# Output copies a unit later, key rounded first in the step, output and value projections between late scores and early transposes

## The reference, cut to what matters

```python
x = x + 0.5 * ffn(layernorm(x))    # router, top 2 of 8 experts, silu, projection, rms norm
x = x + attn(layernorm(x))
x = x + 0.5 * ffn(layernorm(x))
# attn: 16 query heads, 4 key and value heads of 128
q, k = apply_rope(x @ wq.T), apply_rope(x @ wk.T) * key_weights;  v = x @ wv.T
scores = where(causal, -inf, q @ k.T * 128 ** -0.5)
out = (softmax(scores) @ v) @ wo.T
```

## Time and profile before

| what | us |
| --- | --- |
| median of 3 runs | 860.69 |
| lowest, highest | 859.84, 865.01 |
| the profiled execution | 858.07 |
| its span | 856.3 |
| TensorE busy | 787.0 (92%) |
| VectorE busy | 630.1 (74%) |
| ScalarE busy | 531.2 (62%) |
| GpSimd busy | 512.6 (60%) |

### The profile page before, as it was taken

How to read it: one execution, slowest core, us unless ns; L and a number is a source line. 1 busy time by engine, 2 the same in 40 slices (tenths; PEclk the granted TensorE clock), 3 DMA queues, 4 the chain that set the end, 5 groups by cost and what they waited for, 6 DMA issues and landing times.

```text
span 856.3 us, 15659 instructions
## 1 busy us (share of the span) xinstructions
PE 787.0 (92%) x4520; PEld 671.5 (78%) x4520; DVE 630.1 (74%) x1888; ACT 531.2 (62%) x1314; POOL 512.6 (60%) x408
## 2 busy tenths in 40 slices
PE   7899999778999999999999999999999988899996
PEld 4688878657888888878888788887888867788885
DVE  6889895786666766667666676666766677989876
ACT  3565556667667676676766767667676664544543
POOL 4645569764867768677686776867767651103212
PEclk9999999789999999999999999999999999999999
DMA  8235502111123112122211312122121110000001
GB/s 299 94 105 184 198 13 63 26 25 38 26 74 90 32 37 73 37 52 71 73 25 37 105 29 74 37 61 58 41 73 25 38 25 1 1 1 26 1 26 49
DMA packets 30629, 50.11 MB, mean 59 GB/s; under 512 B 3970, under 2 KB 12802, under 8 KB 30594
## 3 DMA queue, kind: packets, MB, share of 16 engines
q1 hardware_dynamic: 30596, 49.71, 20.6%
HBM read 18.76 MB, written 9.96 MB: 34 GB/s over the span
## 4 chain that ended last, share of the span: by engine, by line
POOL 27%; PE 25%; DVE 18%; issue 15%; ACT 12%; DMA 1%; DVEq 1%; POOLq 0%; ACTq 0%; SPq 0%
POOL at_rot L1307 7%; POOL gc L1305 7%; POOL at_rot L1303 6%; POOL at_ql L1295 4%; DVE at_pth L1430 4%; ACT at_pr L1607 3%; ACT at_pr L1598 3%; PE sc L985 3%; PE sc L987 3%; PE sc L986 3%; DVE at_pr L1417 3%; POOL at_keys L1295 2%; DVE at_ptl L1436 2%; DVE f_acc L500 2%; PE pt L1785 1%
## 5 line engine op out<-in xcount | busy, mean ns | idle before, releaser
L1598 ACT ACTIVATE at_pr<-at_pr,at_low 128x512 f32<-128x512 f32 (+7 forms) x256 | 134.5, 526 | 126.5 <-DVE at_low L1417 126.5
L1430 DVE CAST at_pth<-pt 128x512 fp32r<-128x512 f32 x192 | 106.1, 594 | 34.9 <-PE pt L1785 34.8
L1607 ACT ACTIVATE at_pr<-at_pr,at_inv 128x512 f32<-128x512 f32 (+7 forms) x256 | 119.1, 525 | 13.6 <-DVE at_inv L1424 12.1
L1295 POOL TENSOR_TENSOR at_ql<-at_rot,at_qh 128x512 fp32r<-128x512 f32 x64 | 82.6, 1290 | 73.3 <-ACT at_qh L1557 73.3
L1442 DVE TENSOR_TENSOR at_ol<-o,at_oh 128x512 fp32r<-128x512 f32 x64 | 44.1, 689 | 109.3 <-ACT at_oh L1611 109.2
L1305 POOL TENSOR_TENSOR gc<-gc,sin 128x512 f32<-128x512 f32 x80 | 103.7, 1297 | 19.8 <-DMA gc<-ga 19.8
L1307 POOL TENSOR_TENSOR at_rot<-at_rot,gc 128x512 f32<-128x512 f32 x80 | 103.3, 1291 | 6.3
L1417 DVE CUSTOM_DVE_ANT_0 at_pr<-sc,at_mask 128x512 f32<-128x512 f32 (+2 forms) x192 | 91.7, 519 | 19.1 <-PE sc L1772 19.1
L1303 POOL TENSOR_TENSOR at_rot<-ga,cos 128x512 f32<-128x512 f32 x80 | 103.6, 1295 | 2.3 <-POOL at_ql L1295 2.3
L1436 DVE TENSOR_TENSOR at_ptl<-pt,at_pth 128x512 fp32r<-128x512 f32 x192 | 104.9, 587 | 0.0
L1785 PE MATMUL pt<-ident,at_pr 128*128 128x128 f32 x640 | 88.5, 277 | 16.5 <-DVE at_ptl L1436 13.6
(11 more groups left out here) (279 smaller groups left out, 2204.3 us busy)
## 6 DMA issues: line engine op xcount, KB each, us to landing
gc<-ga SPq DMA_DIRECT2D x160, 128.0 KB, 2.3
ga<-in_attn_w SPq DMA_DIRECT2D x8, 384.0 KB, 5.0
at_wo<-attn_split SPq DMA_DIRECT2D x6, 512.0 KB, 4.2
attn_split<-gb SPq DMA_DIRECT2D x6, 384.0 KB, 2.4
attn_split<-gc SPq DMA_DIRECT2D x6, 384.0 KB, 3.3
gb<-attn_split SPq DMA_DIRECT2D x6, 384.0 KB, 3.5
x<-in_x SPq DMA_DIRECT2D x4, 512.0 KB, 8.9
e_raw<-in_expert_w SPq DMA_DIRECT2D x8, 256.0 KB, 5.8
```

The lines of the kernel that those rows point to most:

```text
L1295: pool.tensor_tensor(to, rotated(r), lead.bitcast(F32), ALU.subtract).then_inc(ql_done, 1)
L1430: dve.tensor_copy(pth[kind][:, cols], pt[k % 2][:, 0:FLEN[kind][k]]).then_inc(hi_done, 1)
L1598: act.activation(a, a, ACT.Exp, bias=low[kind][:, k:k + 1], scale=-1.0, accum_out=tot[kind][:, k:k + 1]).then_inc(ex_done, 1)
L1607: act.activation(a, a, ACT.Copy, scale=inv[kind][:, k:k + 1]).then_inc(nm_done, 1)
```

## The change

It reorders. No instruction of the loop is added or removed, no size changes. In each unit from 1 on, ScalarE's `out_lead` of the unit before comes first and VectorE's `out_rest` of the unit before follows the minima; unit 3's own are still taken in unit 3, and its `out_rest` and `value_rest` now come before the late probabilities. `rotated_lead` of the next step's key is ScalarE's first instruction of a step. `raw_out(s + 2, 0)` and `raw_out(s + 2, 1)` come before `normalise`. On TensorE `output_late` moves between the early scores and the late chunk of unit 0, `query(s + 1, 2)` stays behind the scores of unit 1, `value(s + 1)` moves between the scores of unit 2, the early transposes come behind the late chunk, and `value_T` comes before `query(s + 2, 1)`. VectorE takes the first reciprocal before the late chunk's minimum. In the tuple `STEP`, which counts the fills of the banks `pj` by their order, `VT` and `Q1` change places accordingly. Around the loop, `norm_stats(0)` moves behind the first probabilities, GpSimd's `rotate(1, 2)` before `rstd(1)`, and the second network's first part behind the last `out_rest`.

```diff
--- before.py
+++ after.py
@@ -1211,7 +1211,7 @@
         BANK = {K: 1, Q0: 0, Q1: 1, Q2: 1, Q3: 1, V: 0, VT: 0}
         FIRST_BANK = {K: 0, Q0: 1, Q1: 1}
         QFILL = (K, Q0, Q1, Q2, Q3)
-        STEP = ("W1", Q2, "W0", Q3, V, K, Q0, Q1, VT)
+        STEP = ("W1", Q2, "W0", Q3, V, K, Q0, VT, Q1)
         BEFORE = {K: 1, Q0: 2, VT: 3, Q1: 4}
         FULL, BASE = len(STEP), len(BEFORE) + len(STEP) - 2
         TAIL = BASE + FULL * (STEPS - 3)
@@ -1335,8 +1335,10 @@
             rstd(0)
             rest(1, 0)
             rotate(1, 1)
+            rest(1, 1)
+            rotate(1, 2)
             rstd(1)
-            for r in range(2, NR):
+            for r in range(3, NR):
                 rest(1, r - 1)
                 rotate(1, r)
             with pool.Fori(2, STEPS) as s:
@@ -1397,10 +1399,11 @@
                 for kind, c in ((0, 7), (0, 5), (1, 3), (1, 1)):
                     dve.memset(pr[kind][:, columns(c).stop:columns(c).stop + QC], 0.0)
 
-            def mask_min(s, u):
+            def mask_min(s, u, places=range(BT)):
 
                 kind = u % 2
-                for k, c in enumerate(CHUNKS[kind]):
+                for k in places:
+                    c = CHUNKS[kind][k]
                     bank, col = PLACE[c]
                     w = c * QC
                     out, masked = pr[kind][:, columns(c)], mask[:, SEQ - w:SEQ]
@@ -1471,17 +1474,22 @@
                     s2, u2 = following(s, u, 2)
                     more1, more2 = not last or u + 1 < UNITS, not last or u + 2 < UNITS
                     if more2:
-                        mask_min(s2, u2)
+                        mask_min(s2, u2, range(BT) if u % 2 else range(BT - 1))
+                    if u and not (last and u == UNITS - 1):
+                        out_rest(s, u - 1)
+                    if more2 and u % 2 == 0:
+                        inverse(s2, u2, 0)
+                        mask_min(s2, u2, (BT - 1,))
                     if more1:
                         prob_lead(s1, u1, 0)
                         prob_lead(s1, u1, 1)
                     if more2:
-                        inverse(s2, u2, 0)
+                        if u % 2:
+                            inverse(s2, u2, 0)
+                        inverse(s2, u2, 1)
                     if more1:
                         prob_rest(s1, u1, 0)
                         prob_rest(s1, u1, 1)
-                    if more2:
-                        inverse(s2, u2, 1)
                     if first and u in (1, 2):
                         norm_shift(u - 1)
                     if last and u == 2:
@@ -1494,29 +1502,28 @@
                         add_output(s - 1, 1 - u)
                     if last and u == 2:
                         add_last(0)
-                    if u % 2 and more1:
-                        prob_lead(s1, u1, 2)
-                        prob_lead(s1, u1, 3)
-                    out_rest(s, u)
-                    if u == UNITS - 1 and last:
-                        add_last(1)
-                    if last and u == 2:
+                        out_rest(s, 2)
                         hi, lo = first_pair(gb, wa_all)
                         dve.wait_ge(early, 1)
                         dve.wait_ge(raw_done, NR * (STEPS - 1) + 2)
                         dve.tensor_tensor(lo, e_raw[:, 0:2, :], hi.bitcast(F32), ALU.subtract).then_inc(early, 1)
+                        z_rest(*NORMS[2])
+                    if u == UNITS - 1:
+                        out_rest(s, u)
+                    if u == UNITS - 1 and not last:
+                        value_rest(s + 1)
                     if u % 2 and more1:
+                        prob_lead(s1, u1, 2)
+                        prob_lead(s1, u1, 3)
                         prob_rest(s1, u1, 2)
                         prob_rest(s1, u1, 3)
-                    if u == UNITS - 1 and not last:
-                        value_rest(s + 1)
                     if first and u in (1, 2):
                         z_rest(*NORMS[u - 1])
                     if last and u == 0:
                         norm_stats(*NORMS[2])
-                    if last and u == 2:
-                        z_rest(*NORMS[2])
+                    if last and u == UNITS - 1:
                         last_pairs()
+                        add_last(1)
 
             sum_rest(last_block, 1)
             scale_rows(last_block, 0)
@@ -1532,11 +1539,11 @@
             value_rest(0)
             inverse(0, 1, 0)
             inverse(0, 1, 1)
-            norm_stats(*NORMS[0])
             prob_lead(0, 0, 0)
             prob_lead(0, 0, 1)
             prob_rest(0, 0, 0)
             prob_rest(0, 0, 1)
+            norm_stats(*NORMS[0])
             prob_lead(0, 0, 2)
             prob_lead(0, 0, 3)
             prob_rest(0, 0, 2)
@@ -1613,44 +1620,54 @@
             def step(s, first, ahead):
 
                 for u in range(UNITS):
-                    s1, u1 = following(s, u, 1)
                     s2, u2 = following(s, u, 2)
-                    more1, more2 = ahead or u + 1 < UNITS, ahead or u + 2 < UNITS
+                    more2 = ahead or u + 2 < UNITS
+                    if u and (ahead or u < UNITS - 1):
+                        out_lead(s, u - 1)
+                    if first and u > 1:
+                        z_lead(*NORMS[u - 2])
+                    if u == 0 and ahead:
+                        rotated_lead(act, s + 1, 0)
                     if u == 2 and ahead and not first:
                         raw_out(s + 1, 4)
                     if more2:
                         exps(s2, u2, range(2))
-                    if u != 1 and ahead:
-                        rotated_lead(act, s + 1, (0, None, 3, 4)[u])
-                    if more2:
-                        exps(s2, u2, range(2, BT))
-                    if u == 1 and ahead and not first:
-                        raw_out(s + 1, 3)
                     if u == UNITS - 1 and ahead == 2:
                         raw_out(s + 2, 0)
                     if more2:
-                        normalise(s2, u2)
-                    if first and u < 2:
-                        raw_out(s + 1, u + 3)
+                        exps(s2, u2, range(2, 3))
+                    if u == 2 and ahead:
+                        rotated_lead(act, s + 1, 3)
+                    if more2:
+                        exps(s2, u2, range(3, BT))
+                    if u == UNITS - 1 and ahead:
+                        rotated_lead(act, s + 1, 4)
+                    if u == UNITS - 1 and ahead == 2:
+                        raw_out(s + 2, 1)
+                    if u == 1 and ahead:
+                        raw_out(s + 1, 4 if first else 3)
                     if u == (1 if first else 2) and ahead:
                         value_out(s + 1)
+                    if more2:
+                        normalise(s2, u2)
+                    if first and u == 0:
+                        raw_out(s + 1, 3)
                     if first and u in (1, 2):
                         norm_rows(*NORMS[u - 1])
                     if ahead and u < 2:
                         rotated_lead(act, s + 1, u + 1)
-                    if u == UNITS - 1 and ahead == 2:
-                        raw_out(s + 2, 1)
-                    out_lead(s, u)
+                    if not ahead and u == 2:
+                        out_lead(s, 2)
+                        z_lead(*NORMS[2])
+                    if u == UNITS - 1:
+                        out_lead(s, u)
+                    if u == UNITS - 1 and ahead:
+                        value_lead(s + 1)
                     if u == UNITS - 1 and ahead == 2:
                         raw_out(s + 2, 2)
-                    if u == UNITS - 1 and ahead:
-                        value_lead(s + 1)
-                    if first and u in (1, 2):
-                        z_lead(*NORMS[u - 1])
                     if not ahead and u == 0:
                         act.activation(first_pair(gb, wa_all)[0], e_raw[:, 0:2, :], ACT.Copy).then_inc(early, 1)
-                    if not ahead and u == 2:
-                        z_lead(*NORMS[2])
+                    if not ahead and u == UNITS - 1:
                         last_pairs()
 
             act.activation(warm[:, 2], mhalf[:], ACT.Exp)
@@ -1831,26 +1848,26 @@
                     if u == 2 and ahead and not first:
                         query(s + 1, 3)
                     if more2:
-                        scores(s2, u2, range(3) if u2 % 2 == 0 else range(BT))
-                    if u == 1 and ahead and not first:
+                        scores(s2, u2, range(BT) if u % 2 else range(BT - 1))
+                    if u == 0 and first:
                         query(s + 1, 2)
-                    if first and u == 1:
+                    elif u == 0:
+                        output_late(s - 1)
+                    elif u == 1 and first:
                         query(s + 1, 3)
                         value(s + 1)
-                    if u == UNITS - 1 and ahead == 2:
```

(19 more changed lines are left out.)

## The result

| | before | after |
| --- | --- | --- |
| median | 860.45 | **813.25** |
| lowest, highest | 859.84, 865.01 | 811.16, 813.43 |
| the profiled execution's span | 856.3 | 811.3 |

The account below looks back on a forecast made before the run. TensorE was taken to bound the loop. Loop 36.4, step 14 3.4, start 3.4 and step 15 2 summed to 45 us off the profiled 858.1; from the 860.7 median, 815.5, own range 808 to 822, extended to 832.

Parts of the forecast that it names:

- Which stage, and what it loses: Loop, steps 1 to 13, 463 of 856 us: bound by TensorE, which loses time in four waits a step.
- My 2.8 a step: Loop step: 32.8 us of work in 35.6, so 2.8 lost; 36 us over 13 steps, bounds 2.0 and 2.9 a step.
- Idle against starts: Loop: drawn idle undercounts waits; busy time gives 2.0 us a step or 26 in all, instruction starts give 36.
- Key first, cost 0: ScalarE, step start: rounding the key before the exponentials delays nothing, cost 0; without cover 0.6 us a step.
- the rival of the held ScalarE: ScalarE in the loop: a key sum later than about 2.4 us stops its queue; slower, 870 us, chance 0.04.
- Second query, 0.6 to spare: GpSimd's second-query rest ends at 16.8 to 17.0 against scores due at 17.6; the 0.82 us wait goes.
- Output projection as a cover: TensorE, unit 0: `output_late` covers 2.9 us, removing waits of 0.24 and 0.66; needs the value's rest near 0.4.
- Value's transpose: TensorE, unit 3: moved before `query(s + 2, 1)`, its 0.3 us wait goes; the tightest margin, 0.2.
- Copies a unit later: Output copies and rests in the loop: rests end before each `weigh` is due, nearest margin 0.9 us.
- Ends: Outside the loop: step 14 gains 3.4 us, the stretch to step 1 3.4, step 15 2; no change after 738.
- my 2 for step 15: Step 15: three stops for probabilities shrink, the choice of experts comes about 1 us later; gain 2 us, bounds -1 and 4.
- The clock: Two ends granted 0.86 and 0.95: up to 6 us could return in the first if stops shrink; none taken.

Follow-up runs that it names:

- the doubled product: Changed kernel with the cosine product of the second query's rotation done twice on GpSimd, 1.3 to 1.4 us more each step: 825.41 us, ratio 0.958.

## Why the prediction was right, by its steps

- **Which stage, and what it loses.** Right. The loop gave 38.75 of 45.0. My 2.8 a step was 2.98, just above the upper bound of 2.9. The mis-sized term is the work of a step: my pieces add up to 32.86, which I wrote as 32.8, against 32.65. Two of them began right behind a wait and held its restart: unit 2's early scores 1.92, now 1.82 (384.17 to 385.99), and value transpose with late transposes 1.07, now 0.93 (0.35 from 396.71 and 0.58 from 398.53).
- **Idle against starts.** Right. The loop had 2.0 of idle a step and gave 2.98 for four waits. The rule of the Trainium skill (Perfetto Trace Analysis, Identifying the Most-Contended Engine), that matmul busy time is no good measure of the distance, holds here: after the change the loop reads 100% busy, and two experiments lose 0.46 and 0.17 in every step at an empty list of waits. The share of weight loads, which it names instead beside the share of peak operations, went from 82 to 91%, while the step became 8% shorter.
- **Key first, cost 0.** The cost is right, the worth was never priced by itself, and when I did so for the experiment I had it wrong (0 instead of 1.48 a step). It is the largest single part. GpSimd's wait for the key's rounding is 1.11, not about 0: the sum ended at 400.88, 1.8 after the step's start as against my 1.5, and ScalarE waited 1.73 for it, and of the 1.11 the rounding itself is 0.63, which I had left out, the rest is the passing on to ScalarE and back. ScalarE was free early, and the exponential behind the key had to wait another 0.35 for VectorE: the rival of the held ScalarE stayed 0.6 us away from its point (1.8 against 2.4).
- **Second query, 0.6 to spare.** Right: its rest ends 0.98 before the scores start, and the doubled product finds 0.5 to 0.6. Of the difference 0.3 is what passes between a rest's end and the scores' start: 0.29 to 0.30 in each of the loop's 13 waits for this rest before.
- **Output projection as a cover.** Right, and the condition that I named, the value's rest at about 0.4, is what decides: 0.43 in the trace, and without it 1.3 of wait. It covers less than I said when all else is in place: 0.46 a step instead of the 0.24 and 0.66 with their restarts. That VectorE is earlier by then, its first minimum at 2.2 and not 3.1, fits this.
- **Value's transpose.** That the wait goes is right. That this move does it is wrong: the wait went with the key alone, and the move put back costs nothing. The margin was as tight as I said (the query's copy ends at 396.47, the transpose starts at 396.71), but nothing hung on it.
- **Copies a unit later.** I counted no gain and saw no loss. It is 0.17 a step.
- **How the parts add.** Key alone 1.48 a step; everything but the key 1.94 (35.62 to 33.68); together 2.98, less than their sum of 3.42. On top of the rest the key is still worth 1.03.
- **Ends.** Step 14 and 15: 3.1 and 2.1 against 3.4 and 2. To step 1: 2.05 against 3.4, but the profiled execution came later to step 0, in code that the change doesn't touch (its first scores begin at 147.38, before at 146.65). From the first scores to step 1 it is 55.9 against 58.6: 2.8 gained, and 3.5 in the second profile of the changed kernel (55.1). So this term was nearly right. Waits of TensorE there now, 146 to 203.2 us, against the earlier trace rows:

```profile
PE pj L1712 <- ACT z L1583: 4.5, 2, 2.8
PE pt L1802 <- issue: 2.9, 1, 2.9
PE o L1813 <- DVE at_ol L1445: 1.9, 2, 1.6
```

The stops for normalised rows went from 6.7 to 4.5. The 2.9 of the transposes at their issue stood there before as well (146 to 205.3 us):

```profile
PE pt L1785 <- issue: 2.9, 1, 2.9
```

The transposes' 4.7 for VectorE are 0.6 in this profile and 2.3 in the second one: the stop of 1.7 at 160 us is missing in the first, where TensorE was granted the low clock from 154.5 to 161.3, which fits: it came to these transposes later itself. The 1.6 is the wait behind `norm_stats(1)` that I had foreseen. Behind step 15 it is 1.0 longer, where I reckoned no change. All of it arises in the next 17 us. The second network's first split now stands behind the last output's copy on ScalarE, and VectorE waits for it (VectorE before and after; the second network's first product starts at 732.11 and 686.15):

```profile
732.50 1.23 DVE L480 TENSOR_TENSOR f_e_lo<-e_raw,f_e_hi 128x1024 fp32r<-128x1024 f32 x1 [0.45 <-ACT f_e_hi L731]
...
688.22 1.23 DVE L480 TENSOR_TENSOR f_e_lo<-e_raw,f_e_hi 128x1024 fp32r<-128x1024 f32 x1 [1.53 <-ACT f_e_hi L731]
```

So the split comes 1.7 later against that product, and the choice of experts, behind it, 1.0 later (4.71 and 5.74 after the product). TensorE then stops for VectorE for 1.5 us in two places and not 0.7 in one, and its products from there on are 1.0 later to the end. I had foreseen the 1 us, but counted it within my 2 for step 15; against these 2 the two stretches gave 2.1 - 1.0 = 1.1. The cause is read from this order and these waits; no run puts the order back.

- **The clock.** I took none of the 6 us, rightly: 0.88 granted in step 0's stretch, from 0.86, and 0.95 unchanged in step 15's. TensorE still stops there for 1.6 to 2.9 us at a time; in the loop, where no stop is drawn, it is 1.00 as before. The second profile of the changed kernel had 0.94 in step 0's stretch, with stops of 1.4 to 2.9 us, and the stretch was only 0.8 us shorter (55.1 against 55.9). The advice of the Trainium skill (TensorE: Matmul & The Clock Gate, Why this matters for your kernels) against long idle gaps is neither borne out nor refuted by this, since the gaps there have hardly shrunk.

## What to carry to other kernels

When every engine runs its own fixed order, look in each queue for the instruction that waits with others ready behind it, and follow what those others release on the other engines before you take any time as fixed: one rounding moved ahead of two exponentials was worth 23 of the 47 us here. Price a step from starts of instructions that follow no wait, not from busy time or from the list of waits. A cover placed on one engine asks for new inputs: check when the engine that makes them comes to it, and give that engine its new order first.

## What the runs showed of the hardware

A wait of TensorE costs more than its drawn idle: 1.29 idle cost 1.55, 0.77 cost 1.03, 0.51 cost 0.80, so 0.25 to 0.3 more each time in these three kernels. A step can also grow without any idle being drawn: by 0.46 and 0.17 in two others. That short waits are hidden there under the drawn overlap of matmuls is inferred, not shown. And one kernel does not have one clock: the changed kernel was granted 0.88 and 0.94 in the same stretch of step 0, in two executions.
